# Three split tiles instead of two in the second product of a ConvNeXt block (layer 0), with two buffers given up to make room

## What is computed

```python
h = conv_general_dilated(x, conv_w, ..., padding=3, groups=96) + conv_b   # depthwise, 7x7
h = transpose(h, (0, 2, 3, 1))
h = (h - mean(h)) * rsqrt(var(h) + 1e-5) * ln_g + ln_b                    # over channels
h = gelu(h @ w1 + b1)                    # w1: 96 x 384
h = h @ w2 + b2                          # w2: 384 x 96
x = transpose(h) * layer_scale + x
```

## Time and profile before

| | before |
|---|---|
| median of 3 runs | 4337.12 us (4336.25 to 4363.98) |
| the profiled execution | 4339.19 us |
| its span in the trace | 4337.4 us |
| busy over the span: PE, DVE, ACT, POOL | 91%, 79%, 65%, 43% |
| layer 0 in the trace | from 0 to about 1832 us |

### The profile page before, as it was taken

One profiled execution on the slowest core, in us unless ns is written; L12 is line 12 of the kernel. 1 busy time (PEld: TensorE's weight loads), 2 busy tenths in 40 slices (PEclk: granted clock), 3 DMA queues, 4 the chain that ended last, 5 costly groups with the idle time before them and its releaser, 6 DMA issues.

```text
span 4337.4 us, 75304 instructions
## 1 busy us (share of the span) xinstructions
PE 3931.9 (91%) x23254; PEld 2812.4 (65%) x23254; DVE 3446.7 (79%) x5147; ACT 2827.1 (65%) x4720; POOL 1851.3 (43%) x2001
## 2 busy tenths in 40 slices
PE   7999999999999999887989989989889899899898
PEld 6787888888787878684545546556555556455333
DVE  3767666676767675607989989989989899899999
ACT  1545455454636363648787787888788788887765
POOL 0323223232324242405555645646555456455554
PEclk9999999999999999988999989989999899899755
DMA  7565555655565644383424424434333245142000
GB/s 233 145 182 155 171 162 162 174 149 180 137 195 126 210 125 141 80 205 81 103 60 110 106 60 109 97 70 101 80 93 99 63 104 124 46 113 79 16 17 19
DMA packets 315027, 507.50 MB, mean 117 GB/s; under 512 B 190144, under 2 KB 255392, under 8 KB 314288
## 3 DMA queue, kind: packets, MB, share of 16 engines
q1 hardware_dynamic: 314576, 502.08, 43.2%
HBM read 424.94 MB, written 77.07 MB: 116 GB/s over the span
## 4 chain that ended last, share of the span: by engine, by line
issue 18%; DVE 16%; PE 13%; ACT 7%; POOL 2%; DVEq 1%; SPq 0%; ACTq 0%; DMA 0%; POOLq 0%
DVE ps_q L1038 10%; PE ps_front L1238 3%; PE ps_y L1313 3%; DVE u L1060 3%; DVE u L1045 2%; PE ps_c L1288 1%; PE ps_prep L1269 1%; ACT xs L1101 1%; ACT d_a L1137 1%; POOL u L975 1%; DVE q_last L1051 1%; PE ps_y L1310 1%; ACT d_a L1143 1%; PE ps_front L1231 1%; PE ps_prep L1259 1%
## 5 line engine op out<-in xcount | busy, mean ns | idle before, releaser
L518 ACT ACTIVATE act_h<-ps_up,b 128x448 f32<-128x448 f32 x672 | 408.3, 633 | 778.7 <-PE ps_up L636 778.4
L975 POOL TENSOR_TENSOR u<-dxs,b_rows 128x448 f32<-128x448 f32 x672 | 765.2, 1139 | 160.0 <-DVE u L1060 155.2
L1313 PE MATMUL ps_y<-hc,ident 128*128 128x448 f32 x1344 | 748.1, 643 | 0.0
L1060 DVE TENSOR_TENSOR_SCAN u<-d_a,h_last,u 128x448 f32<-128x448 f32 x576 | 691.7, 1201 | 0.0
L1137 ACT ACTIVATE d_a<-delta,log_eps,a_neg 128x448 f32<-128x448 f32 x672 | 507.1, 755 | 260.3 <-DVE u L1060 249.0
L315 POOL TENSOR_TENSOR h_low<-act_h,h_high 128x448 fp32r<-128x448 f32 x224 | 288.3, 1287 | 899.2 <-ACT h_high L523 899.1
L1038 DVE TENSOR_TENSOR_SCAN ps_q<-d_a,q_last,ps_q 128x448 f32<-128x448 f32 x576 | 659.6, 1145 | 0.0
L609 PE MATMUL ps_stage<-win,taps 124*112 124x112 f32 x6144 | 608.3, 261 | 2.7 <-DVE w_low L362 2.7
L609 PEld LDWEIGHTS ps_stage<-win,taps 124*112 124x112 f32 x6144 | 608.1, 178 | 3.3 <-DVE w_low L362 2.8
L1238 PE MATMUL ps_front<-win,taps 120*112 120x112 f32 x4608 | 584.0, 281 | 6.6 <-ACT win L1094 3.7
L1238 PEld LDWEIGHTS ps_front<-win,taps 120*112 120x112 f32 x4608 | 517.7, 189 | 86.3 <-issue 85.0
(11 more groups left out here) (99 smaller groups left out, 7394.3 us busy)
## 6 DMA issues: line engine op xcount, KB each, us to landing
taps<-in_t_dram SPq DMA_DIRECT2D x192, 896.0 KB, 5.0
taps<-in_t_dram SPq DMA_DIRECT2D x192, 672.0 KB, 5.8
xres<-in_x_dram SPq DMA_DIRECT2D x224, 168.0 KB, 2.5
x_dram<-x1o SPq DMA_DIRECT2D x224, 168.0 KB, 2.0
x1pad<-x_dram SPq DMA_DIRECT2D x96, 392.0 KB, 8.5
out_dram<-y SPq DMA_DIRECT2D x168, 224.0 KB
xpad<-in_x_dram SPq DMA_DIRECT2D x29, 1176.0 KB, 10.5
conv<-in_x_dram SPq DMA_DIRECT2D x3, 1176.0 KB, 14.6
```

What stands on the lines that cost most here:

```text
L518: nc.scalar.activation(act_h[u % 2][:, t, :], ps_up[t][:, 0:BT], ACT.Gelu, bias=b1[:, t:t + 1]).then_inc(gelu_done, 1)
L975: nc.gpsimd.tensor_tensor(u[s % U_SLOTS][:, :], dxs[:, t, :], b_rows[n][:, :], ALU.mult).then_inc(u_done, 1)
L1060: nc.vector.tensor_tensor_scan(u[s % U_SLOTS][:, :], d_a[s % DA_SLOTS][:, :], u[s % U_SLOTS][:, :], first, ALU.mult, ALU.add).then_inc(h_d ...
L1313: mm = nc.tensor.matmul(ps_y[:, 0:BT], ident[:, :], hc[s % 2][:, :], start=False, stop=(n == N - 1))
```

## The change

The third tile of the second product is split like the other two (FS goes from 2 to FT = 3). That adds per unit one ACT copy to `h_high`, one POOL subtraction to `h_low`, and puts three float32r products where the one float32 product was, after those of tiles 0 and 1. POOL's new subtraction stands behind its old one. The larger `h_high`, `h_low` and `w2_part` take room: `sq` becomes one buffer, so a square waits until DVE has summed the one before; and w1 is staged in `act_h[1]` until it is split, which is before that buffer's first use.

```diff
-FS = 2
+FS = FT
@@
-        w1 = sb("w1", [C, FF])
@@
-        sq = [sb(f"sq{i}", [TOK, CHUNK, C]) for i in range(2)]
+        sq = sb("sq", [TOK, CHUNK, C])
@@
+        w1 = act_h[1][0:C, 0, 0:FF]
@@
-            def h_low_part(g, u):
-                pool.wait_ge(h_high_ready, (g * UNITS + u) * FS + 2)
-                nc.gpsimd.tensor_tensor(h_low[u % 2][:, 1, :], act_h[u % 2][:, 1, :], h_high[u % 2][:, 1, :],
-                                        ALU.subtract).then_inc(h_low_ready[1], 1)
+            def h_low_part(g, u, t):
+                pool.wait_ge(h_high_ready, (g * UNITS + u) * FS + t + 1)
+                nc.gpsimd.tensor_tensor(h_low[u % 2][:, t, :], act_h[u % 2][:, t, :], h_high[u % 2][:, t, :],
+                                        ALU.subtract).then_inc(h_low_ready[t], 1)

             def unit(g, u):
-                h_low_part(g, u)
+                for t in range(1, FS):
+                    h_low_part(g, u, t)
@@
             def square(g, c):
                 act.wait_ge(ln_centred, g * CHUNKS + c + 1)
-                nc.scalar.activation(sq[c % 2][:, :, :], conv[:, c * CHUNK:(c + 1) * CHUNK, :],
+                if c > 0:
+                    act.wait_ge(ln_ss_ready, g * CHUNKS + c)
+                nc.scalar.activation(sq[:, :, :], conv[:, c * CHUNK:(c + 1) * CHUNK, :],
                                      ACT.Square).then_inc(sq_ready, 1)
@@ down
-                for t in range(FS, FT):
-                    nc.tensor.matmul(ps_down[0:C, 0:BT], w2[:, t, :], act_h[u % 2][:, t, :],
-                                     start=(t == FS), stop=False)
                 for t in range(FS):
                     pe.wait_ge(h_low_ready[t], g * UNITS + u + 1)
                     high, low = h_high[u % 2][:, t, :], h_low[u % 2][:, t, :]
-                    nc.tensor.matmul(ps_down[0:C, 0:BT], w2_part[0][:, t, :], high, start=False, stop=False)
+                    nc.tensor.matmul(ps_down[0:C, 0:BT], w2_part[0][:, t, :], high, start=(t == 0), stop=False)
```

More of the change, by code:

```diff
@@ L393, in ln @@
                     dve.wait_ge(sq_ready, n)
-                    nc.vector.tensor_reduce(ln_ss[k][:, :], sq[k][:, :, :], AX_X, ALU.add).then_inc(ln_ss_ready, 1)
+                    nc.vector.tensor_reduce(ln_ss[k][:, :], sq[:, :, :], AX_X, ALU.add).then_inc(ln_ss_ready, 1)
                 elif step == 4:
```

## The result

The changed kernel took 4481.39 us (median of 6 runs, 4465.27 to 4500.06), the kernel before 4346.38 us (6 runs, 4336.25 to 4373.78): a ratio of 1.0301, 95% interval 1.0257 to 1.0345. It is slower by 3%; the forecast was slower by 103 us, to 4440 us, in a range of 4370 to 4495.

What follows compares the result with a forecast made beforehand. PE looked like the bound, with DVE 10% behind and both tied in a loop. Lost cover and POOL's exclusion of DVE: 13.3 us a group, times 7 groups 93, plus 10 for the last, +103 on 4337.4: 4440 us, range 4370 to 4495.

Steps and rivals of the forecast that it cites:

- The loop of `h_low`, `down`, `residual` and layer norm: PE and DVE wait for each other in every unit; PE's idle time in it was to rise to 15%.
- the signs that were named: New profile: layer 0 about 100 us longer, seven units 37 to 38 us, more PE idle before L649, longer DVE lines.
- PE's own saving: In `down`, three float32r products (0.61 us) replace L644 (0.76 us): 0.15 us a unit, 33 us in all.
- The cover: L644 ran in `down` while `h_low` was awaited; losing that costs up to 0.61 us a unit, about 1.7 an image.
- max(S, H) + 1.84: End of the changed `down`: S is when PE reaches it, H when tile 0's `h_low` is ready; before, max(S + 0.76, H) + 1.22.
- The exclusion: POOL's subtraction and DVE's L401, L386, L390 and L419 block each other for their whole length: most of 3.7 us an image beyond cover.
- The stepping: Seven units, 3 to 10, moved through their new waits: unit 10 starts 4.3 us late, a second image adds 3.6.
- The images: Seven units each: 3.7 us more with window copies, three a group; in the last group 2.5 each, four of them.
- Heads and held units: Per group: first units and the two left 0.6 + 1.0 us, held units, where new work stands in a bare chain, 0.6.
- The clock, the third rival: PE's clock in the units might fall to 0.9 as PE gets less busy: 45 us on top, 4485 us; chance 10%.
- What was costed at nothing: ACT's 224 copies (103 us) hidden in its idle time; single `sq` nothing; staging w1 and splitting w2 under 1 us.
- the row that I went by: Trace at 612.60: POOL's row starts 0.27 us ahead of L401, yet L401 runs undisturbed; the skill's rule would make it wait.

Runs made afterwards that it cites:

- the two kernels that take the change apart: Kernel before with the float32 product last in `down`: ratio 1.0135; changed kernel with tile 2's float32 product at the head of `down`: 1.0189 to the kernel before.
- the kernel with the new work: Changed kernel, keeping its new copies and subtractions, but with tile 2's product in float32 at the head of `down`: 4426.28 us, ratio 1.0189 to the kernel before.

## Why the prediction was right, and where it was too small

- **What bounds the kernel, and the sign.** Right. The loop of `h_low`, `down`, `residual` and layer norm had 10% of slack on DVE, and both parts of the change draw on it. Of the signs that were named, PE idle at L649 (148.9 us) and the longer L402, L387 and L391 came true. Tile 0's subtraction did not grow, and seven units took 38.5 to 41.5 us, more than the 37 to 38 that were named.
- **PE's own saving.** Right in kind: L644's 0.76 us against 0.61 was the only thing that could make the kernel faster. In an image at full clock PE's busy time fell from 33.04 to 32.38 us, 0.66 where the sum had 7 x 0.15. Over the span it fell by 10 us (3931.9 to 3921.9), which says little: kernels here with the same products lie between 3901 and 3950. How much of the saving reached the time is not shown.
- **The cover.** Right, and about the forecast size. The formula max(S, H) + 1.84 gave 1.7 us an image, some 48 us in all; the kernel with the float32 product last paid 55 (59 by the ratio), with 1.98 in that place. Its images are 1.9 us longer.
- **The exclusion.** Right in kind, too small: this is the mis-sized term. The stepping gave it 2.0 us an image, 55 us or so in all; measured apart it is 82 us, or 3.0 us an image. The stepping took it that DVE gets its turn between POOL's two subtractions. In the 24 executions of L402 over 2.0 us it doesn't. The changed kernel's timeline at 463 and at 469 us:

```profile
463.05 2.27 POOL L315 TENSOR_TENSOR h_low<-act_h,h_high 128x448 fp32r<-128x448 f32 x2
463.11 2.93 DVE L402 TENSOR_TENSOR conv<-conv,ln_rstd 112x672 f32<-112x672 f32 x1
...
469.46 2.88 POOL L315 TENSOR_TENSOR h_low<-act_h,h_high 128x448 fp32r<-128x448 f32 x2
469.52 1.80 DVE L402 TENSOR_TENSOR conv<-conv,ln_rstd 112x672 f32<-112x672 f32 x1
```

  At 463 us L402 waits for both subtractions, 2.93 us; at 469 us it waits for one, and POOL's pair takes 2.88 instead of 2.27. Both begin 0.06 us behind POOL. What decides between them the trace does not show.
- **The images.** 3.7 us each were forecast; the 21 images with window copies are 5.1 longer on average (39.4 against 34.3), 107 us where 78 were forecast. In the last group 2.5 was chosen between 1.2 and 3.7; it was 4.7, 9 us in all. The upper bound there was the other images' value, which was itself too low.
- **Heads and held units.** 2.2 us a group forecast, 18.2 - 15.3 = 2.9 measured. PE waits there for POOL's second subtraction, as the sum had it:

```profile
620.80 0.45 PE L649 MATMUL ps_down<-h_high,w_high 128*96 128x448 f32 x1 [0.25 <-POOL h_low L315]
...
625.55 0.45 PE L649 MATMUL ps_down<-h_high,w_high 128*96 128x448 f32 x1 [0.65 <-POOL h_low L315]
```

- **The clock, the third rival.** It holds in small. Of the 21 images, 13 have a stretch of 3.4 us at the lower clock, one of them two, and so have all three images measured in the last group; before, none has. In the image from 448.5 us it follows PE's longest wait:

```profile
474.40 0.42 PE L649 MATMUL ps_down<-h_high,w_high 128*96 128x448 f32 x1 [1.83 <-DVE h_low L420]
...
475.06 0.57 PE L649 MATMUL ps_down<-h_high,w_high 128*96 128x448 f32 x1
475.80 0.57 PE L651 MATMUL ps_down<-h_low,w_high 128*96 128x448 f32 x1
476.17 0.57 PE L649 MATMUL ps_down<-h_high,w_high 128*96 128x448 f32 x1
```

  From 475.06 on, products start 0.37 us apart instead of 0.20, the lower of TensorE's two levels (1.2 instead of 2.4 GHz). That image is 1.3 us longer than its neighbours. Ten of the 13 are 1.2 to 2.8 us longer than the 38.7 us of most images at full clock, 15 us in all. The other three took 38.5 or 38.6 us, so a slow stretch can also cost nothing; the second line of windows below is nearly all of such an image. These 15 us are an estimate from the windows; no run took them apart. Without them the 21 images would still be 14 us over the forecast. In the last group every image has such a stretch, so no price can be read there. In the two kernels that take the change apart no image has one; outside the images, the kernel with the new work spent more time at the lower clock than before (92 us against 61 from 150 us to the end of layer 0), so a part of its 82 us may be clock. A wait of the same length in a first image left the clock at 1.00, so the length of one wait does not decide it:

```profile
674.52 0.42 PE L649 MATMUL ps_down<-h_high,w_high 128*96 128x448 f32 x1 [1.82 <-DVE h_low L420]
...
648.00:686.70 38.70, 32.45 (x187) 27.14 (x186) 33.30 (x49) 31.52 (x58) 26.72 (x20) 1.00 0.41 94
686.70:725.00 38.30, 33.77 (x186) 28.03 (x185) 33.36 (x49) 31.34 (x57) 25.54 (x19) 0.96 0.41 95
```

- **What was costed at nothing.** ACT's copies and the two buffers: right, 1.0010 and 0.9990.
- **The time.** +103 was forecast against +135 in the span and 3.01% by the runs. The mechanism was the forecast one; of the 43 us that layer 0 lost beyond the forecast, 29 lie in the images with window copies, 9 in the last group's, 5 in heads and held units. That the whole lies nearer (32 us over) is luck: layer 1 took 10 us less. How much of the 29 and 9 is arbitration and how much the clock is not taken apart beyond the estimate above.
- **The rule of the Trainium skill on the port pair** ("SBUF — State Buffer", section "Who interferes with whom"). By it the sum would have been 9 us more, at one place; how its 0.45 us a unit come about the prediction doesn't show. The runs agree with the exclusion that it states: DVE's means grow with the length of POOL's subtraction, and are near before's with a quarter of its columns. But neither its statement that the first to issue keeps the ports nor the row that I went by gives the whole picture: with the same 0.06 us between the starts, DVE was let in once between POOL's two, and once not.

## What to carry to other kernels

Before an instruction at the head of a group of dependent work is replaced by one that waits, look at what it covers: here a slower product that waits for nothing was worth more than a faster one behind a wait, and the cheapest gain was to put the operand that comes last at the end of the accumulation. Work put on an idle POOL is not free for DVE: count the DVE instructions with operands in SBUF that can meet it, and expect to pay what they are lengthened by, which can grow much faster than POOL's own work does. When two engines hand work to each other in a loop, neither's busy share is the bound; step through one period by hand, with the worse arbitration as its upper end.

## What was new about the hardware

- The price of POOL's second subtraction is far from proportional: 0, 112, 224, 448 columns cost 4, 5, 19 and 82 us in all, at 0, 0.43, 0.67 and 1.16 us of POOL each. It goes with how often a DVE operation (the multiplication by `ln_rstd`) waits for both subtractions: 3, 19 and 33 times of 128 for 112, 224 and 448 columns.
- A DVE operation can wait for two POOL instructions in a row (2.93 us where 0.84 is its own), and for one in the same situation 6 us later (1.80 us).
- A subtraction of 0.64 us on DVE (mean; DVE starts its next instruction 0.54 us later where nothing holds it) cost no more in the whole than one of 1.16 us on an otherwise half idle POOL (1.0087 against 1.0126).
